# Layer 0 of a four-layer block: the products with the values at every other step, an operand buffer split off, the next batch's set-up moved

## The reference, cut to what matters

```python
scores = jnp.einsum('bhqd,bhkd->bhqk', q, k) / scale
c2p = jnp.take_along_axis(c2p_att, c2p_pos, axis=-1)      # query x embedding of the distance
p2c = jnp.swapaxes(jnp.take_along_axis(p2c_att, p2c_pos, axis=-1), -1, -2)   # key x embedding
probs = jax.nn.softmax(scores + (c2p + p2c) / scale, axis=-1)
ctx = jnp.einsum('bhqk,bhkd->bhqd', probs, v)
out = ctx @ Wo + bo + hidden_states                       # then a layernorm with scale and bias
x = x + out + xn @ sign(weight).T
```

## Time and profile before

| what | before |
|---|---|
| median of 3 runs | 2317.31 us (2316.05 to 2317.94) |
| the profiled execution | 2315.2 us |
| its span | 2313.4 us |
| PE busy | 1962.6 us (85% of the span) |
| DVE busy | 1762.3 us (76%) |
| ACT busy | 1438.2 us (62%) |
| POOL busy | 1203.9 us (52%) |
| first and last exponential of layer 0 | start at 78.3 and 958.7 us |

### The profile page before, as it was taken

One profiled execution on the slowest core, in us unless ns is written; L12 is line 12 of the kernel. 1 busy time (PEld: TensorE's weight loads), 2 busy tenths in 40 slices (PEclk: granted clock), 3 DMA queues, 4 the chain that ended last, 5 costly groups with the idle time before them and its releaser, 6 DMA issues.

```text
span 2313.4 us, 38686 instructions
## 1 busy us (share of the span) xinstructions
PE 1962.6 (85%) x13526; PEld 1477.2 (64%) x13526; DVE 1762.3 (76%) x4100; ACT 1438.2 (62%) x2795; POOL 1203.9 (52%) x900
## 2 busy tenths in 40 slices
PE   3789898988989898777986999999998467888898
PEld 2466566656665665455674777778777345566798
DVE  8687878787878788557277888888887799873486
ACT  2577777777777776533324666666665257765575
POOL 3777676776767666227352444445443365425400
PEclk9999999999999999969998999999999689999999
DMA  3888788887878786220100000000000000002100
GB/s 108 286 305 277 262 274 267 271 266 263 278 256 277 264 278 237 70 83 1 36 1 5 1 1 1 1 1 1 1 1 21 11 1 1 1 1 88 32 2 37
DMA packets 73874, 264.13 MB, mean 114 GB/s; under 512 B 12272, under 2 KB 32240, under 8 KB 73168
## 3 DMA queue, kind: packets, MB, share of 16 engines
q1 hardware_dynamic: 72304, 254.31, 33.3%
q10 hardware_dynamic: 1376, 7.34, 0.8%
HBM read 140.30 MB, written 121.31 MB: 113 GB/s over the span
## 4 chain that ended last, share of the span: by engine, by line
PE 37%; DVE 9%; ACT 6%; issue 2%; POOL 2%; DMA 0%; POOLq 0%; ACTq 0%; DVEq 0%; SPq 0%
PE PS L157 9%; PE PS L161 7%; PE PS L163 7%; PE PS L162 7%; PE PS L326 7%; ACT AR L167 2%; DVE AR L181 2%; ACT L167 1%; DVE PT L181 1%; DVE DR L181 1%; ACT AR L171 1%; DVE AR L200 1%; DVE AR L185 1%; ACT PT L171 1%; DVE AR L193 1%
## 5 line engine op out<-in xcount | busy, mean ns | idle before, releaser
L167 ACT ACTIVATE AR<-PS,AR 128x512 f32<-128x512 f32 x1008 | 686.2, 687 | 297.7 <-DVE AR L193 145.1
L193 DVE TENSOR_REDUCE AR<-PS 128x1 f32<-128x512 f32 x896 | 616.2, 688 | 118.8 <-PE PS L163 99.9
L326 PE MATMUL PS<-ident,AR 128*128 128x128 f32 x3816 | 589.0, 279 | 81.5 <-ACT AR L171 38.9
L157 PE MATMUL PS<-AR 128*64 128x128 f32 (+7 forms) x4190 | 509.7, 361 | 107.9 <-DVE AR L181 43.8
L326 PEld LDWEIGHTS PS<-ident,AR 128*128 128x128 f32 x3816 | 435.3, 142 | 247.5 <-ACT AR L171 98.6
L181 POOL TENSOR_TENSOR AR<-AR 128x1024 f32<-128x1024 f32 (+5 forms) x246 | 370.3, 1521 | 278.7 <-DVE AR L181 133.4
L157 PEld LDWEIGHTS PS<-AR 128*64 128x64 f32 (+4 forms) x4190 | 291.7, 133 | 273.6 <-issue 126.1
L171 ACT ACTIVATE AR<-PS 128x512 f32<-128x512 f32 (+3 forms) x612 | 355.3, 586 | 112.9 <-PE PS L157 49.9
L176 POOL TENSOR_SCALAR AR<-AR 128x512 f32<-128x512 f32 x144 | 245.5, 1705 | 292.8 <-DVE AR L1564 219.6
L181 DVE TENSOR_TENSOR PS<-PS,AR 128x192 f32<-128x192 f32 (+1 forms) x512 | 202.1, 395 | 157.6 <-PE PS L525 151.8
L171 ACT ACTIVATE PT<-PS 128x512 fp32r<-128x512 f32 x320 | 191.4, 598 | 208.6 <-PE PS L326 171.7
(11 more groups left out here) (157 smaller groups left out, 2994.5 us busy)
## 6 DMA issues: line engine op xcount, KB each, us to landing
scr<-AR SPq DMA_DIRECT2D x128, 800.0 KB, 4.3
XN<-scr SPq DMA_DIRECT2D x85, 768.0 KB, 6.2
AR<-scr SPq DMA_DIRECT2D x43, 768.0 KB, 6.3
AR<-qsc SPq DMA_DIRECT2D x96, 192.0 KB
qsc<-AR SPq DMA_DIRECT2D x96, 128.0 KB, 3.5
AR<-in_wgu SPq DMA_DIRECT2D x16, 256.0 KB, 3.3
X<-in_x ACTq DMA_DIRECT2D x1, 2048.0 KB, 8.5
AR<-in_wi ACTq DMA_DIRECT2D x1, 2048.0 KB, 8.2
```

What stands on the lines that cost most here:

```text
L157: return pe.e.matmul(out, lhsT, rhs, start=start, stop=stop)
L167: return ac.e.activation(out, in_, func, bias=bias, scale=scale, accum_out=accum)
L193: return dv.e.tensor_reduce(out, in_, AX.X, ALU.max, negate=True)
L326: return pe.e.transpose(out, in_, ident[0:k, 0:k])
```

## The change

The products with the values of a group run at steps 16G+21, +23, +25, +27 instead of four in a row; `ptb` holds six heads instead of five; the copy of the result moves from 16G+25 to 16G+28. The operand for the keys above the far step leaves the group's buffer: it has two buffers of its own, `OPU`, and its own two DMAs (`load_upper`), issued at step 2 of a group for the next group, while the other four stay at step 6 for the group after the next. `TMP` has one buffer instead of two, and POOL makes each of its halves by itself (128x512), 4.5 heads ahead. Set-up of the next batch starts at step 1 of a batch: q and k at r = 1 and 3, far and g0 at 13 and 15, v at 35; ACT's splits at 5, 8, ..., 20, POOL's at 7, 10, ..., 22, SP's writes at 13, 19, 25. The ends of the batch before move to heads 17, ct 19, mo 29, sw 31, root 34, norm 36, sum 38, last 48; `HEADS` to 33, 47, 62.

```diff
-        ptb = A0.take(5, 4, 512)
+        PTN = 6
+        ptb = A0.take(PTN, 4, 512)
...
-        OP = [[A0.take16(4, 512) for _ in range(3)] for _ in range(OPN)]
+        OP = [[A0.take16(4, 512) for _ in range(2)] for _ in range(OPN)]
+        OPU = [A0.take16(4, 512) for _ in range(2)]
...
-        TMP = [A0.take(2, 4, 128) for _ in range(2)]
+        TMP = A0.take(2, 4, 128)
...
+        opu = [sem(f"l0_opu{k}") for k in range(2)]
-        STEPS0 = 4 * NBH + 20
-        AHEAD = {"q": 13, "k": 15, "far": 17, "g0": 19, "v": 31}
-        HEADS = (33, 42, 58)
-        ENDS = [{"heads": 10, "ct": 25, "mo": 27, "sw": 29, "root": 31, "norm": 33, "sum": 37, "last": 42}] * NB
-        ENDS += [{"heads": 10, "ct": 12, "mo": 14, "sw": 15, "root": 17, "norm": 18, "sum": 19, "last": 20}]
+        STEPS0 = 4 * NBH + 28
+        AHEAD = {"q": 1, "k": 3, "far": 13, "g0": 15, "v": 35}
+        XF_OUT = {2: "q", 4: "k", 14: "far", 16: "g0"}
+        SPLIT_AT = 5
+        HEADS = (33, 47, 62)
+        ENDS = [{"heads": 17, "ct": 19, "mo": 29, "sw": 31, "root": 34, "norm": 36, "sum": 38, "last": 48}] * NB
+        ENDS += [{"heads": 14, "ct": 16, "mo": 18, "sw": 19, "root": 21, "norm": 22, "sum": 23, "last": 25}]
         def small(u):
...
         def loaded(en, G):
-            en.wait_ge(opl[G % OPN], 96 * (G // OPN + 1))
+            en.wait_ge(opl[G % OPN], 64 * (G // OPN + 1))
+        def loaded_u(en, G):
+            en.wait_ge(opu[G % 2], 32 * (G // 2 + 1))
         def l0_pe(pe):
...
-                OQ, OL, OU = OP[G % OPN]
+                (OQ, OL), OU = OP[G % OPN], OPU[G % 2]
+                loaded_u(pe, G)
...
-                    ins = mm(pe, OB[32 * hh:32 * hh + 9, :], VA[b % 2][:, jb, g * 4 + hh, :], ptb[:, (4 * G + hh) % 5, jb, :],
+                    ins = mm(pe, OB[32 * hh:32 * hh + 9, :], VA[b % 2][:, jb, g * 4 + hh, :], ptb[:, (4 * G + hh) % PTN, jb, :],
...
-                if 0 <= G < 4 * NB and r < 4:
-                    pv(G, r)
+                if 0 <= G < 4 * NB and r in (0, 2, 4, 6):
+                    pv(G, r // 2)
         def l0_dv(dv):
...
             def pattern(k):
-                for x in range(3):
+                for x in range(2):
+                if k < 2:
+                    ts(dv, flat(OPU[k]), zero, pat[:, 2:3], None, ALU.add).then_inc(op_init, 1)
...
             def g_out(n, x):
-                dv.wait_ge(p_cr, n + 1)
+                dv.wait_ge(p_cr, 2 * n + x + 1)
-                step = TMP[n % 2][:, x]
+                step = TMP[:, x]
...
-                        ac.wait_ge(p_cr, 16 * (b - 1))
+                        ac.wait_ge(p_cr, 2 * 16 * (b - 1))
...
             def p_out(v):
-                if n >= 5:
-                    ac.wait_ge(pv_mm, (n - 5) // 4 + 1)
-                copy(ac, ptb[:, n % 5, :, ib * 128:ib * 128 + 128], quarters(PS[:, 3 + v % 2, :])).then_inc(to_a, 1)
+                if n >= PTN:
+                    ac.wait_ge(pv_mm, (n - PTN) // 4 + 1)
+                copy(ac, ptb[:, n % PTN, :, ib * 128:ib * 128 + 128], quarters(PS[:, 3 + v % 2, :])).then_inc(to_a, 1)
             def os_out(G):
...
-                    if r in (14, 16, 18, 20):
-                        xf_out(("q", "k", "far", "g0")[r // 2 - 7], b + 1)
-                    if r in (15, 18, 21, 24, 27, 30):
-                        split_ac(b + 1, (r - 15) // 6, (r - 15) // 3 % 2)
-                G, k = divmod(u - 25, 16)
+                    if r in XF_OUT:
+                        xf_out(XF_OUT[r], b + 1)
+                    k, late = divmod(r - SPLIT_AT, 3)
+                    if 0 <= k < 6 and late == 0:
+                        split_ac(b + 1, k // 2, k % 2)
+                G, k = divmod(u - 28, 16)
...
-            def corr(n):
+            def corr(n, x):
-                step = G0A[b % 2][:, :, :, h:h + 1]
+                step = G0A[b % 2][:, x, :, h:h + 1]
-                if n >= 2:
-                    po.wait_ge(g_o, 2 * (n - 1))
-                tt(po, TMP[n % 2], bc(steps.unsqueeze(2), [128, 2, 4, 128]), bc(step, [128, 2, 4, 128]), ALU.mult).then_inc(p_cr, 1)
+                if n >= 1:
+                    po.wait_ge(g_o, 2 * (n - 1) + x + 1)
+                tt(po, TMP[:, x], bc(steps[:, x].unsqueeze(1), [128, 4, 128]), bc(step, [128, 4, 128]), ALU.mult).then_inc(p_cr, 1)
             def own_band(n):
...
-            for n in range(5):
-                corr(n)
+            for n in range(4):
+                corr(n, 0)
+                corr(n, 1)
+            corr(4, 0)
-                if ib == 1 and n + 5 < NBH:
-                    corr(n + 5)
+                if ib == 0 and n + 4 < NBH:
+                    corr(n + 4, 1)
-                if b + 1 < NB and r in (17, 20, 23, 26, 29, 32):
-                    split(b + 1, (r - 17) // 6, (r - 17) // 3 % 2)
+                if ib == 2 and n + 5 < NBH:
+                    corr(n + 5, 0)
+                k, late = divmod(r - SPLIT_AT - 2, 3)
+                if b + 1 < NB and 0 <= k < 6 and late == 0:
+                    split(b + 1, k // 2, k % 2)
...
+                    loaded_u(sp, 4 * (b - 2) + 2)
+                    loaded_u(sp, 4 * (b - 2) + 3)
...
+            def rows(G, k):
+                return bass.AP(qsc.tensor, G // 4 % 2 * QSZ + k * 16 * 48 * 512 + G % 4 * 2048, [[8192, 48], [1, 2048]])
+            def far_rows(G, k, n):
+                at = G // 4 % 2 * QSZ + 2 * 16 * 48 * 512 + (32 * (k // 2) + 8 * (G % 4) + k % 2) * 1536
+                return bass.AP(qsc.tensor, at, [[512, n], [3072, 4], [1, 512]])
             def load_group(G):
-                b, g = divmod(G, 4)
-                o, base, done = OP[G % OPN], b % 2 * QSZ, opl[G % OPN]
-                far_row = lambda k: base + 2 * 16 * 48 * 512 + (32 * (k // 2) + 8 * g + k % 2) * 1536
-                rows = lambda k: bass.AP(qsc.tensor, base + k * 16 * 48 * 512 + g * 2048, [[8192, 48], [1, 2048]])
-                sp.wait_ge(qw[b % 2], 208 * (b // 2 + 1))
-                sp.wait_ge(op_init, 3 * min(G + 1, OPN))
+                o, done = OP[G % OPN], opl[G % OPN]
+                sp.wait_ge(qw[G // 4 % 2], 208 * (G // 8 + 1))
+                sp.wait_ge(op_init, (2, 5, 8)[min(G, 2)])
-                sp.e.dma_start(flat(o[0][0:48]), rows(0)).then_inc(done, 16)
-                sp.e.dma_start(o[0][48:54], bass.AP(qsc.tensor, far_row(0), [[512, 6], [3072, 4], [1, 512]])).then_inc(done, 16)
-                for x in (1, 2):
-                    sp.e.dma_start(flat(o[x][0:48]), rows(1)).then_inc(done, 16)
-                    sp.e.dma_start(o[x][54:57], bass.AP(qsc.tensor, far_row(1 + x), [[512, 3], [3072, 4], [1, 512]])
-                                   ).then_inc(done, 16)
+                sp.e.dma_start(flat(o[0][0:48]), rows(G, 0)).then_inc(done, 16)
+                sp.e.dma_start(o[0][48:54], far_rows(G, 0, 6)).then_inc(done, 16)
+                sp.e.dma_start(flat(o[1][0:48]), rows(G, 1)).then_inc(done, 16)
+                sp.e.dma_start(o[1][54:57], far_rows(G, 2, 3)).then_inc(done, 16)
+            def load_upper(G):
+                sp.wait_ge(qw[G // 4 % 2], 208 * (G // 8 + 1))
+                sp.wait_ge(op_init, (3, 6)[min(G, 1)])
+                if G >= 2:
+                    sp.wait_ge(s_mm, 16 * (G - 1))
+                sp.e.dma_start(flat(OPU[G % 2][0:48]), rows(G, 1)).then_inc(opu[G % 2], 16)
+                sp.e.dma_start(OPU[G % 2][54:57], far_rows(G, 3, 3)).then_inc(opu[G % 2], 16)
             def write(n):
...
+            load_upper(0)
...
-                if b + 1 < NB and r in (22, 28, 34):
-                    q_write(b + 1, (r - 22) // 6)
+                if b + 1 < NB and r in (13, 19, 25):
+                    q_write(b + 1, (r - 13) // 6)
+                if u % 16 == 2 and u // 16 + 1 < NBH // 4:
+                    load_upper(u // 16 + 1)
...
-            en.wait_ge(p_cr, NBH)
+            en.wait_ge(p_cr, 2 * NBH)
```

## The result

| what | before | after |
|---|---|---|
| median | 2316.77 us (4 runs, 2316.05 to 2317.94) | 2278.51 us (4 runs, 2277.15 to 2280.80) |
| after / before, 95% interval | | 0.9835 [0.9818, 0.9852] |
| the profiled execution, its span | 2315.2, 2313.4 us | 2277.15, 2275.3 us |
| first and last exponential of layer 0 | 78.3 and 958.7 us | 76.1 and 922.0 us |

The change makes the kernel 38 us faster; 45 were forecast. Between the first and the last exponential of layer 0 lie 845.9 us instead of 880.4 (34.4 less), the first comes 2.2 us earlier, and what follows the last takes 1353.3 us instead of 1354.7. So the gain is where it was looked for, in the steps.

The account below looks back on a forecast made before the run. No single engine bounds a batch: DVE fills quiet steps, PE the block of products. Terms 21 + 19 + 4 + 1 = 45 us off 2315.2 give 2270.2, forecast as a median of 2272 us; range 2246 to 2304.

Parts of the forecast that it names:

- the spread of the products: In each group's products stretch: one `pv` per pair of steps uses PE's spare time; 0.65 us a group, 21 us.
- The signs named for it: In the trace if right: pairs of 3.2 us, PE never idle, no ACT wait for `pv`, POOL's 128x1024 gone.
- One sign of being wrong: DVE's `g_out` or `add` waiting for POOL, or POOL for a DMA, by more than 1 us a batch.
- The rival of a delay that stays behind each single `pv`: In the new stretch PE idles 0.32 us after each `pv`: eight steps 14.12 us, 2313 us; chance 0.09.
- Of the 1.32 us of leftover I take 0.6 for it: Behind the block of products: six heads in `ptb` end ACT's 0.70 us wait; 0.6 us a group, 19 us.
- the wait was free: ACT's 0.70 us wait behind the block is slack, only 26 us come: 2291 us; chance 0.10.
- The projections, ... stood at steps without `pv` and do so again: 0: Set-up and ends of a batch: moved between steps without `pv`, costed at 0.
- The 4 us for the split copies: ACT's split copies in set-up: one fewer in quiet steps, 7 x 0.635 = 4 us, between 0 and 13.
- The late reads: SP's query-row writes delay the table reads behind them: up to 69 us, 2341 us, slower; chance 0.08.
- the batch's stall: PE's stall at DVE's normalisation shrinks and its slow clock goes: 2.7 us a batch, 19 us, 2253 us; chance 0.15.
- The halves of `corr`: POOL, with one `TMP`: each half 1.161 us, cost 0 by cover; if that fails, up to 1.2 us a head.
- The start: PE's wait for the first loads: four tables needed instead of six, 1 us gained, between 0 and 2.86.

Follow-up runs that it names:

- e1: Changed kernel with the four products with the values in a row again (steps 16G+21 to +24), all else kept: 2302.49 us.
- e2: e1 with ACT's `p_out` waiting as with five heads in `ptb` and the result's copy back at 16G+25: 2296.68 us.
- e8: e1 with only the result's copy back at 16G+25, six heads in `ptb` and no wait: 2300.46 us.
- e9: Kernel before with only `heads` moved, from steps 10, 33, 42, 58 to 14, 33, 47, 62: 2328.45 us.
- e11: Kernel before with the set-up early as in e10 and `heads` moved to 17, 33, 47, 62: 2303.29 us.
- e10: Kernel before with only the next batch's set-up early (q 1, k 3, far 13, g0 15, splits and writes; v stays at 31): 2317.58 us.
- e5: Changed kernel with norm at step 38 instead of 36 and sum at 40 instead of 38: 2271.07 us.
- e4: Changed kernel with the first six writes of query rows at step 14, behind the read, instead of 13: 2275.36 us.
- e3: Changed kernel with the set-up late again (q 13, k 15, far 18, g0 21, splits from 15 and 17, writes at 22, 28, 34): 2304.82 us.
- e13: e12 with root at 37, norm at 40, sum at 42 and last at 46: 2281.04 us.
- e12: Changed kernel with three moves: first query-row write at 14, norm 38 with sum 40, last statistics at 44 instead of 48: 2262.66 us.

## Why the prediction was right, and which step failed

**Right: the direction, the place and the size.** 2278.5 us lies 6.5 above the forecast of 2272 and well within the range of 2246 to 2304. The gain is in the steps of layer 0.

**Right: the spread of the products,** 21 us forecast, 24 by e1 and 21 by its groups. The eight steps took 12.93 us for 12.84. The signs named for it are in the trace: pairs of 3.1 us, PE never idle in them, no wait of ACT for the products, POOL's 128x1024 gone. Each came, and yet one of them, ACT's wait, carried no time. Batches of 107.2 to 109.1 us lie partly above the 106 to 108 named, since groups 0 to 2 did not follow the quiet one. One sign of being wrong came as well: POOL waits for the tables read back by far more than 1 us a batch longer (56.2 us in all for 19.4). The rival of a delay that stays behind each single `pv` did not come: its eight steps would have taken 14.12 us.

**Failed: "Of the 1.32 us of leftover I take 0.6 for it".** The 0.70 us wait of ACT was given 19 us; e1, e2 and e8 show that it was slack. This was the rival "the wait was free", with 0.10, and it held for this term. The leftover of 1.32 us was taken as the wait's because 0.70 fitted into it, though `heads` stood in the same 1.32 us. By e9, 0.43 of it is the place of `heads`; e1 shows that another 0.44 goes with the spread (1.09 gained, for 0.65 in the sum).

**Failed: moves costed at nothing.** "The projections, ... stood at steps without `pv` and do so again: 0" asked only whether a step was free of `pv`, and not how far it stood from the next user of the shared bank. The moves of set-up and heads together are worth 12 us (e11), apart they lose 12 and 1 (e9, e10). The 4 us for the split copies were not found in e10. So 24 us were forecast for all but the spread (19, 4 and 1) and 13 to 14 came, mostly for a reason that was not in the sum. That the total still came out near the forecast is luck in this half of it: a term of 19 us that was not there, and one of 12 us that was not counted. The same nothing hid a loss: moved from r = 33 to 36, the normalisation stands beside a longer part of POOL's `own_band`, and it takes 3.63 us where it took 2.52 before (told at e5).

**Partly true: two rivals.** The late reads came as described, but small: about 6 us in the profile by e4's steps, 3 in the medians, in place of the 69 of the rival. The set of six at r = 13 cost 0 to 3 us in a batch, below 1 us in five of seven; the one at r = 19 was moved in e3 alone, together with the rest of the set-up. And the batch's stall lost its slow clock. Before, PE waited 2.60 us and ran 3.50 us at 0.53, about 1.2 GHz; now the waits are 1.40 and 1.43 us, and in most batches the clock stays at 1.00 behind them. The rival asked 2.7 us a batch for it; group 2 didn't get shorter at all (29.12 to 29.36), since the idle time of PE was only divided, 2.83 in two for 2.60 in one, the normalisation got 1.1 us longer, and v came into the group (35 for 31). How the clock's gain and these losses make up the 0.24 us was not taken apart. The prediction also read the earlier trace rows wrongly: PE stands still behind the normalisation (348.69 to 351.22) and not before it ends, while DVE catches up with what the steps need. The Trainium skill, TensorE: Matmul & The Clock Gate, HAM oscillation, says that it is PE's idle stretches that bring the half rate; the traces agree for the most part, with 2.60 and 2.23 us ahead of a slow stretch (before, e13) and 1.41 us in a batch of e12, whose six inner batches have no slow stretch. But they don't settle it: in one batch each of e9 and e13 no slow stretch follows a wait of 2.6 or 2.2 us, and in the changed kernel's batch 1 one follows waits of 1.41 and 1.43.

**Right, small terms.** The halves of `corr` are free with one `TMP`: DVE waits for POOL once in 790 us for 1.0 us and once for 0.6. A half takes 1.05 us where 1.161 was taken. The start came 1.2 us earlier on PE (58.07 for 59.30 in the earlier trace rows) and 2.2 us at the first exponential, for 1 forecast.

**Left open.** e1 is 13 us faster than before and e11 is 12; what lies between them (operands apart, `corr` in halves, ends later) is at most a few us in either direction and was not priced piece by piece. Products at every other step with only five heads in `ptb` were not tried: the copy of head 4G+5 would wait for a product that stands behind it.

## What to carry to other kernels

When a resource is full in one stretch and idle in its neighbour, spread the work that fills it: the gain can be read from two rows (the pair's busy time and the idle time of a quiet pair). A wait in the trace next to unexplained time is not its cause until it has been put back alone; here the wait stayed and the time went. Steps of a hand-written order that share one buffer are moved as a set, with the distance between its users checked first. And look at how long a moved piece of work takes at its new place, since a neighbour can stretch it: here the same normalisation took 2.11, 2.52 or 3.63 us.

## What the hardware showed that was not expected

**The lower clock comes and goes, and hides effects of 3 us.** Before has one stretch of about 3.4 us at a clock near 0.5 in seven of its eight batches; the changed kernel's profile has three in layer 0, e4's six, e12's two and none in its six inner batches, e13's one in seven of its eight batches. Two batches of e4 and a slow stretch in the first of them, columns as in the earlier trace rows:

```profile
279.57:389.39 109.82, 98.87 (x846) 70.25 (x845) 91.82 (x198) 82.36 (x146) 81.19 (x74) 0.97 0.81 275
389.39:496.63 107.24, 95.89 (x846) 68.37 (x845) 91.68 (x198) 82.50 (x146) 80.24 (x74) 1.00 0.83 281
345.50:349.00 3.50, 3.50 (x17) 1.33 (x17) 2.39 (x5) 2.19 (x4) 3.34 (x4) 0.54 0.62 232
```

The same instructions take 109.82 us with two slow stretches and 107.24 with none, 1.3 us for each. Three such stretches more than in the changed kernel, 4 us, can take back most of what e4 gained. Why they come in e4 in some batches and not in others, with the same order of instructions, is not settled. The spread of the changed kernel's own batches, 107.2 to 109.1 us, is of the same size (the one of 109.05 shown above has a clock of 0.98).

**A small multiplication of DVE ended with POOL's, in every batch.** The first multiplication of the normalisation (128x4, from and to AR) takes 0.16 us in e5 and e12, where POOL is idle. In the changed kernel and e13 it takes 1.67 to 1.75 us, beside POOL's 128x768 of `own_band` (in one batch of each it is the second multiplication that does), and in the kernel before 0.56 to 0.57 us in six batches and 1.17 in the last. In all seven batches of each of these three kernels it ends within 0.03 us of the end of POOL's multiplication. DVE's row maximum, which reads PSUM, is not stretched: at 342.27 in the changed kernel it takes its usual 0.69 us beside the same work of POOL. No run moved POOL's work alone, so the cause rests on these coinciding ends. The profile counts the time as busy and shows no wait, so it is found only by the length of the instruction.

**A multiplication on POOL with broadcast operands was not dearer than other work of that size.** A half of `corr` multiplies two operands that are both broadcast and takes 1.05 us. The 128x512 operations beside it in the earlier trace rows took 1.161 us (the subtraction of a split) and 1.276 (the last sum's multiplication and addition), and the plain addition of the last sum takes 1.27 in the changed kernel. Two halves cost 2.1 us against 1.914 for the whole, so a split costs 0.19 us a head, less than half of the 0.41 that was allowed for.
